# Attention pipeline of a four-layer block on one core: shift rows in the scores' bank, and another order of the fourth pair's steps

## The reference

```
# layer 0 (layer 1 has 64 value channels, no Wo, and adds x + out)
q = Wq x + bq; k = Wk x + bk; v = Wv x + bv      # q, k: 8 channels; v: 32
attn = softmax(q^T k, axis=-1)                    # 256 x 256 for each image
x = gamma * (Wo (v attn^T) + bo) + x
# layer 2
out = conv3x3(relu(bn(x)), E0 * sign(w0)); out = conv3x3(relu(bn(out)), E1 * sign(w1)); x = out + x
# layer 3: 4 x 4 covariance over groups of channels, Cholesky, triangular solve, weights, bias
```

## Time and profile before

| | us |
|---|---|
| median of 3 runs (67.15 to 68.71) | 67.28 |
| profiled execution | 67.17 |
| its span, first to last instruction | 65.4 |
| TensorE busy | 56.9 (87%) |
| VectorE busy | 46.2 (71%) |
| ScalarE busy | 42.5 (65%) |
| POOL busy | 21.8 (33%) |

### The profile page before, as it was taken

The page is one execution under the profiler, slowest core; times in us unless marked ns, Lnnn a source line. Parts: engine busy times, 40 slices in busy tenths (PEclk is TensorE's granted clock), DMA queues, the critical chain, the costliest instruction groups (busy, mean ns, idle before and its releaser), DMA issues. The chain is left out here.

```text
span 65.4 us, 2158 instructions
## 1 busy us (share of the span) xinstructions
PE 56.9 (87%) x811; PEld 35.6 (54%) x811; DVE 46.2 (71%) x120; ACT 42.5 (65%) x138; POOL 21.8 (33%) x64
## 2 busy tenths in 40 slices
PE   5987898889999998995989898999899999999900
PEld 2332443557465635542436385599658998854500
DVE  0079899596757989996693856998478978576520
ACT  0710198999999499969999495680049445268620
POOL 5000863730373705775032108318212050054000
PEclk9999999999999999999999999999999999999999
DMA  0887970000000000000000000000000000000053
GB/s 0 234 242 133 318 319 13 0 0 10 0 0 0 5 0 0 0 10 10 0 0 0 0 10 0 0 0 10 0 0 0 10 0 10 0 0 0 0 193 128
DMA packets 2457, 2.71 MB, mean 41 GB/s; under 512 B 400, under 2 KB 2064, under 8 KB 2448
## 3 DMA queue, kind: packets, MB, share of 16 engines
q1 hardware_dynamic: 2160, 2.39, 11.8%
q10 hardware_dynamic: 288, 0.20, 1.0%
HBM read 2.06 MB, written 0.52 MB: 39 GB/s over the span
## 5 line engine op out<-in xcount | busy, mean ns | idle before, releaser
L711 PE MATMUL bank<-const-bfloat16-1.0 128*64 128x512 bf16 x64 | 9.2, 429 | 0.8 <-PEq L1379 0.8
L552 ACT ACTIVATE probs<-bank 128x512 f32<-128x512 f32 x16 | 8.8, 603 | 1.1 <-PE bank L794 1.1
L532 ACT ACTIVATE bank<-bank,negmax 128x256 f32<-128x256 f32 x20 | 9.1, 461 | 0.2 <-DVE negmax L1085 0.2
L833 PE MATMUL both<-probs,vt 128*64 128x256 f32 x56 | 7.6, 387 | 0.3 <-DVE cut L1095 0.3
L1085 DVE TENSOR_REDUCE negmax<-bank 128x2 f32<-128x512 f32 x10 | 6.7, 685 | 1.4 <-PE bank L770 0.8
L366 POOL TENSOR_TENSOR cut<-cut 64x256 f32<-64x256 f32 x7 | 4.3, 611 | 8.3 <-DVE cut L1095 5.3
L532 ACT ACTIVATE both<-both,negmax 128x256 f32<-128x256 f32 x12 | 5.4, 452 | 1.5 <-DVE negmax L1085 1.5
L941 PE MATMUL bank<-hi,taps 64*64 64x225 f16 (+2 forms) x126 | 5.9, 267 | 0.1
L941 PE MATMUL bank<-lo,taps 64*64 64x225 f16 (+2 forms) x126 | 5.9, 265 | 0.0
L711 PEld LDWEIGHTS bank<-const-bfloat16-1.0 128*64 128x64 bf16 x64 | 3.7, 119 | 3.7 <-issue 1.6
L941 PEld LDWEIGHTS bank<-hi,taps 64*64 64x64 bf16 x126 | 5.0, 107 | 0.6 <-issue 0.4
(11 more groups left out here) (154 smaller groups left out, 122.7 us busy)
## 6 DMA issues: line engine op xcount, KB each, us to landing
cw<-conv_w SPq DMA_DIRECT2D x2, 288.0 KB, 4.7
x<-x_in SPq DMA_DIRECT2D x4, 128.0 KB, 2.9
out<-res SPq DMA_DIRECT2D x4, 128.0 KB, 1.9
kst<-consts SPq DMA_DIRECT2D x1, 428.0 KB, 5.4
aw<-attn_w ACTq DMA_DIRECT2D x1, 128.0 KB, 2.7
aw<-attn_w SPq DMA_DIRECT2D x1, 128.0 KB, 4.0
half<-select SPq DMA_DIRECT2D x1, 96.0 KB, 2.7
kst<-consts SPq DMA_DIRECT2D x1, 64.5 KB, 4.0
```

Of the source, the lines that this page charges most:

```text
L532: nc.scalar.activation(part, part, ACT.Exp, bias=negmax[:, i % 2, n:n + 1], accum_out=total[:, i % 2, n:n + 1]).then_inc(total_out, 1)
L552: nc.scalar.activation(probs[:, i % 2, g], pb_t[g][:].rearrange("p (t n) -> p t n", t=CH), ACT.Exp).then_inc(exp_out, 1)
L711: mm(bank[lanes(h)], filler[:, lanes(h)], filled, start=True, stop=True)
L833: last = mm(mixed(i)[g * C:(g + 1) * C], vt[:, i % 2, t, g * C:(g + 1) * C], probs[:, i % 2, g, t, :], start=(t == 0 and i < ITERS - 1), s ...
```

## The change

- The rows of pair i go to the bank of the pair's second scores, pb_s[(2i + 1) % 3], whose reader is done by then, instead of the right half of the value bank. With that, values no longer waits for rows_out, and shifts_to_rows no longer for v_out and rows_out. The wait for part0_out of the first pair moves from shifts_to_rows(0) to values(0).
- scores(i) waits for rows_out (i - 1), that is for shift_rows(i - 2), since its first image overwrites the bank in which those rows lie.
- TensorE's order: shifts_to_rows(2) goes behind mix(1). scores(4), shifts_to_rows(3), scores_t(3) and mix(2) go ahead of values(3), in this order; add_shifts(3) goes behind values(3) and ahead of replicate(5).
- VectorE's order: values_out(3) goes from behind first_parts(5) to behind queries_keys(5).

```
--- before.py
+++ after.py
@@ -202,7 +202,6 @@
                  ctx.enter_context(nc.psum_tensor(f"bank{n}", [P, HALF], F32)) for n in range(8)]
         GROUPS = 6 * PAIRS
         pb_rep, pb_v, pb_pv = banks[0], banks[1], banks[3]
-        pb_rows = pb_v[:, N:2 * N]
         pb_s, pb_t = [banks[n] for n in (2, 4, 5)], banks[6:8]
         pb_conv = [[banks[n] for n in ns] for ns in ((0, 1, 4, 5), (6, 7, 2, 0))]
         pb_small = banks[3]
@@ -288,6 +287,10 @@
 
             return pb_pv[:, 0:N] if i < ITERS - 1 else pb_rep[:, 0:N]
 
+        def rows_of(i):
+
+            return pb_s[(2 * i + 1) % 3][:, 0:N]
+
         def lanes(g):
 
             return slice(g * C, (g + 1) * C)
@@ -557,7 +560,7 @@
                 act.wait_ge(rows_mm, i + 1)
                 if i >= 2:
                     act.wait_ge(t_mm, 2 * (i - 1))
-                nc.scalar.activation(shift_t[:, i % 2, :], pb_rows, ACT.Identity).then_inc(rows_out, 1)
+                nc.scalar.activation(shift_t[:, i % 2, :], rows_of(i), ACT.Identity).then_inc(rows_out, 1)
 
 
             first_bias()
@@ -739,14 +742,14 @@
                                   start=True, stop=True)
                 last.then_inc(rep_mm, 1)
 
-            def values(i, rows_done):
+            def values(i):
                 wait_x(pe, i)
                 if i >= 1:
 
                     pe.wait_ge(v_out, i)
-                pe.wait_ge(rows_out, rows_done)
                 if i == 0:
                     pe.wait_ge(wv0_set, 1)
+                    pe.wait_ge(part0_out, PAIRS)
                 wv = wv0[:] if i < PAIRS else aw[:, A_V1:A_V1 + P]
                 for t in range(CH):
                     for h in range(2):
@@ -760,6 +763,8 @@
                 pe.wait_ge(qk_out, i + 1)
                 if i == 0:
                     pe.wait_ge(k0_out, 1)
+                if i >= 2:
+                    pe.wait_ge(rows_out, i - 1)
                 for g in range(G):
                     unit = 2 * i + g
                     if unit >= 3:
@@ -795,18 +800,13 @@
                        shift_t[rows, i % 2, :].unsqueeze(1).to_broadcast([C, CH, N]),
                        start=False, stop=True, skip_group_check=True).then_inc(t_mm, 1)
 
-            def shifts_to_rows(i, values_done):
+            def shifts_to_rows(i):
+
                 pe.wait_ge(shift_out, i + 1)
-
-                if i == 0:
-                    pe.wait_ge(part0_out, PAIRS)
-                if i >= 1:
-                    pe.wait_ge(v_out, values_done)
-                    pe.wait_ge(rows_out, i)
                 tops = shift[:, i % 2].bitcast(BF16)
                 for u in range(CH):
                     for h in range(2):
-                        last = mm(pb_rows[lanes(h), u * P:(u + 1) * P], tops[:, u, P * h + 1:P * (h + 1):2],
+                        last = mm(rows_of(i)[lanes(h), u * P:(u + 1) * P], tops[:, u, P * h + 1:P * (h + 1):2],
                                   half[:, 0, :], start=True, stop=True)
                 last.then_inc(rows_mm, 1)
 
@@ -850,60 +850,60 @@
             scores(1)
             replicate(2)
             keep_warm(WARM_START[2], pb_pv)
-            shifts_to_rows(0, 0)
+            shifts_to_rows(0)
             value_weights()
             scores(2)
             add_shifts(0)
-            values(0, 1)
+            values(0)
             replicate(3)
-            values(1, 1)
+            values(1)
             mix(0)
-            shifts_to_rows(1, 2)
+            shifts_to_rows(1)
             scores_t(1)
             scores(3)
             add_shifts(1)
             project(4)
-            values(2, 2)
+            values(2)
             scores_t(2)
-            shifts_to_rows(2, 3)
             mix(1)
+            shifts_to_rows(2)
             replicate(4)
             add_shifts(2)
             project(5)
-            values(3, 3)
             scores(4)
+            shifts_to_rows(3)
             scores_t(3)
-            shifts_to_rows(3, 4)
             mix(2)
+            values(3)
+            add_shifts(3)
             replicate(5)
-            add_shifts(3)
             project(6)
             scores(5)
             mix(3)
-            values(4, 4)
+            values(4)
             replicate(6)
             project(7)
-            shifts_to_rows(4, 5)
+            shifts_to_rows(4)
             scores_t(4)
             scores(6)
             add_shifts(4)
-            values(5, 5)
-            shifts_to_rows(5, 6)
+            values(5)
+            shifts_to_rows(5)
             replicate(7)
             scores_t(5)
             add_shifts(5)
             scores(7)
             mix(4)
             last_shortcut()
-            shifts_to_rows(6, 6)
+            shifts_to_rows(6)
             scores_t(6)
             add_shifts(6)
-            values(6, 7)
+            values(6)
             mix(5)
-            shifts_to_rows(7, 7)
+            shifts_to_rows(7)
             scores_t(7)
             add_shifts(7)
-            values(7, 8)
+            values(7)
             mix(6)
             mix(7)
 
@@ -1165,11 +1165,11 @@
             add_shortcut(1)
             queries_keys(4)
             first_parts(5)
-            values_out(3)
             maxima(4, 0)
             maxima(4, 1)
             add_shortcut(2)
             queries_keys(5)
+            values_out(3)
             first_parts(6)
             maxima(5, 0)
             maxima(5, 1)
```

## The result

The changed kernel takes 69.17 to 69.31 us where the kernel before takes 67.15 to 67.36; the ratio is 1.0291 (95% interval 1.0266 to 1.0316), 1.9 to 2.0 us slower. The forecast was 68.9, the whole range 67.9 to 69.5.

What follows compares the result with a forecast made beforehand. ScalarE's queue was taken to bound the kernel, gapless from exps(4). The delays put exps(4) and the end 1.66 us late: span 65.4 to 67.06, 68.8 with 1.77 around it, 68.9 against the median; whole range 67.9 to 69.5.

Steps and rivals of the forecast that it cites:

- ScalarE, not TensorE, is the pacemaker: Before exps(4): ScalarE sets the pace, with stalls of 0.54 and 0.85 us from TensorE's order; gapless from 28.78.
- shifts_to_rows(2) behind mix(1): Pair 2: rows wait for mix(1), so ScalarE idles 0.81 us before shift_rows(2), which comes 1.06 late.
- The old stall of 0.85 has moved forward and the pair is 0.40 late: Pair 3: ScalarE's stall before shift_rows(3) now falls earlier; shift_rows(3) starts at 22.77 instead of 22.37.
- values(3) and add_shifts(3) ahead of replicate(5): TensorE behind mix(2): values(3) takes 0.50 us, add_shifts(3) 0.32, making queries_keys(5) 1.37 late.
- scores(6) behind shift_rows(4): Pair 4: add_shifts(4) comes a scores group later, 0.24 us of pure delay before exps(4), bounds 0 and 0.40.
- scores(2) behind shift_rows(0): Start of attention: the wait makes VectorE's image 0.09 us later, 0.07 reaching shift_rows(1), bounds 0 and 0.33.
- values_out(3) on VectorE: Between queries_keys(5) and first_parts(6): a copy of 0.34 us, putting maxima(5,0) 1.34 behind queries_keys(5), before 1.24.
- The spare time before totals(5,0): ScalarE, pair 5: under 0.1 us to spare behind maxima(5,0), so 1.47 late there gives 1.42 late at totals(5,0).
- A small stall at shift_rows(2): Rival: ScalarE doesn't lose 0.8 us at shift_rows(2); exps(4) only 0.84 late, 68.1 us; chance 0.22.
- Not slower: Rival: the 0.85 us before shift_rows(3) go, less 0.24 for scores(6), giving 66.7 us; chance 0.06.
- The fall of the clock: Rival: TensorE's 0.8 us idle stretch halves its clock to 1.2 GHz, up to 2.6 us more, 71.5; chance 0.04.
- Changes between matmuls of 64 and of 128 rows: TensorE, project(5) to project(6): six changes instead of four, about 0.1 us each, already in the steps.

Runs made afterwards that it cites:

- experiment 9: Kernel before, with the new bank for pairs 2 and 3 only, mix(1) ahead of scores_t(2), shifts_to_rows(3) ahead of scores_t(3): 67.09 to 67.31 us, ratio 0.9997.
- Experiment 3: Changed kernel with shifts_to_rows(2) put back ahead of mix(1): 68.20 and 68.21 us, ratio 1.0141 to the kernel before.
- experiment 2: Kernel before, rows still in the value bank, with the new order on TensorE and VectorE: 68.52 and 68.63 us, ratio 1.0196.
- experiment 4: Changed kernel with values(3) between scores(4) and shifts_to_rows(3) instead of behind mix(2): 68.63 to 68.80 us, ratio 1.0217.
- experiment 1: Changed kernel with the old order on TensorE and VectorE, so the new bank and its waits alone: 67.43 and 67.62 us.
- experiment 5: Changed kernel with add_shifts(1) ahead of scores(3) and add_shifts(4) ahead of scores(6): 68.71 to 68.85 us, ratio 1.0227.
- experiment 7: Changed kernel with values_out(3) ahead of queries_keys(5) on VectorE: 68.82 to 69.28 us, ratio 1.0264.
- experiment 8: Changed kernel with add_shifts(1), (4) ahead of scores(3), (6), shifts_to_rows(2) ahead of mix(1), values(3) behind project(6), values_out(3) behind first_parts(6): 67.69 to 67.80 us, ratio 1.0068.
- experiment 6: Changed kernel with shift_rows(2) behind totals(3,1) on ScalarE: 70.11 to 70.22 us in one session, 68.77 to 68.85 us when run again.

## Why the prediction had the mechanism right, and where its sum fell short

- **What bounds it, and the direction.** Right behind exps(4): ScalarE's unbroken run from there carried the delay to the end unchanged, 1.99 us at exps(4), 2.00 at shift_rows(7), and the tail added nothing. Ahead of exps(4) "ScalarE, not TensorE, is the pacemaker" says too much: in experiment 9 ScalarE's stall before shift_rows(3) fell from 0.85 to 0.44 and nothing was won, since TensorE's list was full. The 0.85 at which the change aimed was not there to be had by earlier rows alone.
- **shifts_to_rows(2) behind mix(1): right in mechanism and size.** Forecast 1.06 late, 0.81 of standing still; measured 1.29 late, of which 0.13 is the start, with 0.70 of standing still (the rest because totals(3,0) was itself later). Experiment 3 shows that it is the largest single cause, 0.83, and experiment 2 that it needs no new bank.
- **"The old stall of 0.85 has moved forward and the pair is 0.40 late": right.** 0.61 late, 0.48 without the start.
- **values(3) and add_shifts(3) ahead of replicate(5): right in mechanism, a little too small.** queries_keys(5) was forecast 1.37 late and is 1.65, or 1.52 without the start; undoing values(3) alone gave 0.45 (experiment 4).
- **scores(6) behind shift_rows(4): right**, forecast 0.24, measured 0.25 (experiments 1 and 5).
- **scores(2) behind shift_rows(0): the term that failed most.** The prediction took 0.09 at the maxima and 0.07 at shift_rows(1), the latter from no row. Measured, without the start, are 0.13 at the maxima (12.89 - 11.92 against 12.63 - 11.79) and 0.17 at shift_rows(1) (16.34 - 11.92 against 16.04 - 11.79). From shift_rows(0) to shift_rows(1) it is 4.41 to 4.43 us in all nine traces with this wait and 4.25 in the three without it, so the 0.17 is the wait's. Between the two lie values_out(0), values(1) and mix(0); values(1) is already the whole 0.17 late.
- **values_out(3) on VectorE: its 0.34 counted as lengthening a distance from 1.24 to 1.34; the distance is 1.33.** That was right, and experiment 7 shows why it was cheap: without the copy VectorE waits for scores(5), and 0.07 is all that is won.
- **Where the sum failed.** It gave 1.6 us against the median before, and 1.96 was measured (0.0291 of 67.28). In the stretch itself it is 1.66 forecast and 1.87 measured. Three terms were too small, by 0.22 together, and that is the miss of 0.21 but for rounding:
  - The wait of scores(2): 0.07 at shift_rows(1), measured 0.17.
  - The way from mix(2) to replicate(5): 1.70 (22.99 to 24.69), measured 1.78. Of this, 0.05 is values(3): the prediction read its 0.50 where replicate(6) followed it, and ahead of add_shifts(3) it takes 0.55 (24.11 to 24.66).
  - The spare time before totals(5,0): 0.05 by the sum, measured about 0.01. totals(5,0) starts 0.77 behind maxima(5,0) where it waits for them (26.77 to 27.54), and before it started 0.78 behind them.
- **Steps between engines.** TensorE's scores started 0.11 and 0.10 us after ScalarE's end, not the 0.06 read off one row (28.24 to 28.30). But their four matmuls held the queue for 0.21 instead of 0.24, which all but makes up for it.
- **The two halves.** Split by experiment 2, the order costs 1.28 instead of 1.17 and the waits of the scores 0.59 instead of 0.49. What is left between 1.87 and 1.96 is less than the scatter of the start, and no step of the change explains it.
- **The rivals.** A small stall at shift_rows(2) is out: it is 0.70 and worth 0.83. "Not slower" is out, and for the reason given: maxima(5,0) had no time to spare. In the mended kernel of experiment 8 just this wait is what eats the earlier rows. The fall of the clock is out too: the granted clock is full (2.4 GHz) through the changed stretch and until 66.4 us, and about half (1.2 GHz) in the 1.0 us that is left. TensorE's last matmul ended at 64.2, so the fall costs nothing. It is the last slice of this line:

```profile
PEclk9999999999999999999999999999999999999997
```

- **Changes between matmuls of 64 and of 128 rows.** scores_t(2) to mix(1), with a change, takes 0.33 us (18.59 to 18.92), and scores(3) to add_shifts(1), matmuls of the same shape and number without one, 0.21 (16.83 to 17.04): 0.12 for the change, near the 0.1 of the prediction. Behind a mix it is 0.12 as well (1.03 in experiment 4 against 0.91), if nothing else lies between. The Trainium skill (TensorEngine Tiling (Array Packing), Key Properties) says that changing the tiling mode drains TensorE, which agrees; it names no price, so the prediction's 0.2 for two more changes is the trace's 0.1 twice. Here they add nothing that can be seen: one falls in TensorE's wait for the shifts of pair 3, the other lies between rows(3) and scores_t(3), 0.23 (22.64 to 22.87) where the prediction took 0.24. What a change behind a group of rows costs stays open, since rows(3) to mix(2), without one, took 0.23 in the kernel before and 0.14 in experiment 1.

## What to carry to other kernels

When a producer is moved behind a long step on one engine, look up where its reader stands in the other engine's list: here one step of 0.3 us moved behind a mix of 0.9 stopped ScalarE for 0.7, with totals(3,1), logs(3) and exps(2) queued behind, and undoing it gave 0.83 of 1.87. A buffer that frees one wait brings a wait for its next writer; put that writer behind whatever the critical engine waits for, not ahead (add_shifts before scores gave 0.38). And a stall on the pacing engine is worth removing only if what it does next isn't due from elsewhere: experiments 8 and 9 cut the stall of 0.85 to 0.17 and 0.44 and did not beat the kernel before, since TensorE's list, already full, set the next meeting point.

## What the runs showed of the hardware

In experiment 6 all four executions of one session were 1.4 us longer than those of another, the same kernel. The trace shows TensorE's matmuls longer up to about 9.5 us of the span: project(3) took 1.07 us where the changed kernel's took 0.60, and each matmul of scores(0) 0.39 to 0.42 instead of 0.27 to 0.28. This line is the late one's:

```profile
7.37 1.07 PE L725 MATMUL bank<-x,aw 128*64 128x256 f32 x4
```

The late trace of experiment 9 shows the same, with 1.07 us for project(3). The granted clock of this stretch is given as full in all of them, so here only the durations show that TensorE was slow; why it was is not shown. An execution that is late for this reason can still be used if distances are taken from a point behind it: 26.47 and 26.48 in the two.
